# A graph network layer on one core: the matmul loop without its peeled steps, and loads that wait for the quad three ahead

## The reference, cut to what matters

```
agg = segment_sum(edge_attr, dst, num_segments=12500)      # 200000 x 128 f32, dst sorted
h = maximum(layernorm(x), 0)                               # 12500 x 128 f32
h = relu(concat(h, agg) @ W1 + b1)
h = relu(h @ W2 + b2)
h = h @ W3 + b3
out = x + layernorm(h) * ln_w + ln_b
```

## Time and profile before

| | us |
|---|---|
| median of three runs | 317.98 |
| the profiled execution, its own time | 318.58 |
| its span | 316.8 |
| PE busy | 271.7 (86%) |
| DVE busy | 246.4 (78%) |
| first load issued | 0.74 |
| flag known, branch taken | about 19.8 |
| last edges issued | 293.68 |
| last output issued | 313.76 and after |

### The profile page before, as it was taken

The page is one execution under the profiler, slowest core; times in us unless marked ns, Lnnn a source line. Parts: engine busy times, 40 slices in busy tenths (PEclk is TensorE's granted clock), DMA queues, the critical chain, the costliest instruction groups (busy, mean ns, idle before and its releaser), DMA issues.

```text
span 316.8 us, 12734 instructions
## 1 busy us (share of the span) xinstructions
PE 271.7 (86%) x3927; PEld 185.0 (58%) x3927; DVE 246.4 (78%) x944; ACT 149.6 (47%) x407; POOL 179.0 (56%) x208
## 2 busy tenths in 40 slices
PE   2949998998998888888988888889888888898991
PEld 0726666665665566655665565656655656565570
DVE  4946588989787878877787888778777887878885
ACT  1442555555544445455444454554443545544632
POOL 8636555566555656655555656555556565555431
PEclk9978999999999999999999999999999999999998
DMA  7999999999999999999999999999999999999994
GB/s 245 343 380 371 372 373 372 373 373 373 373 373 373 373 374 373 373 373 373 378 381 378 382 380 379 379 383 379 380 381 379 382 381 380 380 383 380 383 397 153
DMA packets 81855, 116.50 MB, mean 368 GB/s; under 512 B 5712, under 2 KB 81840, under 8 KB 81840
## 3 DMA queue, kind: packets, MB, share of 16 engines
q1 hardware_dynamic: 80826, 115.86, 103.2%
q10 hardware_dynamic: 1014, 0.46, 0.5%
HBM read 109.90 MB, written 6.40 MB: 367 GB/s over the span
## 4 chain that ended last, share of the span: by engine, by line
SPq 55%; PE 14%; issue 12%; DMA 11%; DVE 6%; ACT 0%; DVEq 0%; POOL 0%; POOLq 0%
SPq L295 43%; DMA ring<-in_edge_attr 9%; PE part_ps L438 6%; SPq L322 5%; SPq L290 5%; PE place_ps L449 3%; DMA dst_i<-in_dst 1%; PE hid_ps L466 1%; SPq L331 1%; PE hid_ps L483 1%; PE hid_ps L473 1%; PE y_ps L489 1%; DVE onehot L878 1%; DVE local L900 1%; DVE least L898 1%
## 5 line engine op out<-in xcount | busy, mean ns | idle before, releaser
L800 POOL TENSOR_SCALAR place<-iota,rows_at 128x128 f32<-128x128 f32 x131 | 104.9, 804 | 104.2 <-PE place_ps L449 95.0
L438 PE MATMUL part_ps<-ring,onehot 128*32 128x128 f32 x3120 | 113.4, 279 | 26.7 <-DMA ring<-in_edge_attr 25.8
L438 PEld LDWEIGHTS part_ps<-ring,onehot 128*32 128x32 f32 x3120 | 78.4, 110 | 72.6 <-issue 50.1
L954 DVE TENSOR_TENSOR agg<-place_ps,agg 128x128 f32 x131 | 38.0, 290 | 50.8 <-PE place_ps L449 49.0
L449 PE MATMUL place_ps<-place,part 128*128 128x128 f32 (+1 forms) x262 | 64.4, 328 | 2.6 <-POOL place L800 2.3
L808 POOL TENSOR_TENSOR xs<-xs,vecs 128x384 f32 (+2 forms) x33 | 54.8, 1662 | 19.4 <-ACT h L669 19.4
L878 DVE TENSOR_TENSOR onehot<-iota,local_t 128x768 f32<-128x768 f32 x66 | 63.5, 963 | 0.3 <-issue 0.3
L655 ACT ACTIVATE part<-part_ps 128x128 f32<-128x128 f32 x131 | 35.0, 268 | 48.4 <-PE part_ps L438 46.8
L449 PEld LDWEIGHTS place_ps<-place,part 128*128 128x128 f32 (+1 forms) x262 | 39.8, 190 | 29.1 <-issue 22.1
L669 ACT ACTIVATE h<-xs,x_shift,x_rstd 128x128 f32 (+2 forms) x98 | 41.3, 483 | 2.4 <-DVE x_shift L871 2.4
L685 ACT ACTIVATE hid<-hid_ps,b1s 128x384 f32<-128x384 f32 (+1 forms) x33 | 19.0, 577 | 45.4 <-PE hid_ps L473 45.4
(11 more groups left out here) (86 smaller groups left out, 201.9 us busy)
## 6 DMA issues: line engine op xcount, KB each, us to landing
ring<-in_edge_attr SPq DMA_DIRECT2D x260, 384.0 KB, 8.8
xs<-in_x SPq DMA_DIRECT2D x32, 192.0 KB, 8.5
out_x<-xs SPq DMA_DIRECT2D x11, 384.0 KB
out_x<-xs SPq DMA_DIRECT2D x16, 72.0 KB
dst_i<-in_dst SPq DMA_DIRECT2D x1, 768.0 KB
out_x<-xs SPq DMA_DIRECT2D x8, 48.0 KB
ring<-in_edge_attr SPq DMA_DIRECT2D x1, 192.0 KB, 8.7
out_x<-xs SPq DMA_DIRECT2D x1, 192.0 KB
```

What stands on the lines that cost most here:

```text
L438: last = nc.tensor.matmul(part_ps[par_q % 2][s * WIN:(s + 1) * WIN, 0:D], onehot[:, oct_par, first + s, j, :], e[:, s, j * D:(j + 1) * D], ...
L800: nc.gpsimd.tensor_scalar(place[:, par_q % 2, :], iota[:, 0:P], rows_at[:, k:k + 1], None, ALU.is_equal).then_inc(place_ready, 1)
L954: nc.vector.tensor_tensor(v, place_ps[par_q % 2][:, 0:P], v, ALU.add).then_inc(added, 1)
```

## The change

PE's loop takes steps 0 to 29 in 15 rounds, and no step stands alone. For this, DVE raises `y_evacuated` by one at the start, and those that wait for it wait for one more. Ahead of the branch, PE waits for the last copy of `local_t` and does 20 matmuls of 32 rows' columns into a bank that nothing reads. SP's loop is cut in two: steps 1 to 4 as they were, and steps 5 to 12, in which SP waits, ahead of each quad's two loads, until the quad three before has landed on all engines, and raises a semaphore that nobody waits for.

```
+UNDERWAY = 3
+SPARE = 20
+LEVEL_FROM = 2
...
+                    def few_underway(turn, pairs):
+
+                        n = turn - UNDERWAY
+                        sp.wait_ge(edges_loaded[n % RING], LANDED * (pairs + n // RING + 1))
+                        sp.sem_inc(sp_went_on, 1)
...
                         load_x(i + XAHEAD, (par + XAHEAD) % 2, pairs + (par + XAHEAD) // 2)
                         for k in range(4):
+                            if level:
+                                few_underway(4 * par + RING + AHEAD + k, pairs)
                             reload(4 * i + RING + AHEAD + k, (4 * par + AHEAD + k) % RING)
...
-                    with sp.Fori(0, ROUNDS - STORED_EARLY) as t:
+                    with sp.Fori(0, LEVEL_FROM) as t:
                         step(2 * t + 1, 1, t)
                         step(2 * t + 2, 0, t + 1)
+                    with sp.Fori(LEVEL_FROM, ROUNDS - STORED_EARLY) as t:
+                        step(2 * t + 1, 1, t, level=True)
+                        step(2 * t + 2, 0, t + 1, level=True)
...
-                    pe.wait_ge(y_evacuated, g)
+                    pe.wait_ge(y_evacuated, g + 1)
...
+                pe.wait_ge(local_t_ready, ROWT)
+                for _ in range(SPARE):
+                    nc.tensor.matmul(hid2_ps[0:WIN, 0:WIN], ident[:, 0:WIN], ident[:, 0:WIN], start=True, stop=True)
...
-                    step(0, 0, 0)
-                    with pe.Fori(0, (STEPS - 3) // 2) as t:
+                    with pe.Fori(0, (STEPS - 1) // 2) as t:
+                        step(2 * t, 0, t)
                         step(2 * t + 1, 1, t)
-                        step(2 * t + 2, 0, t + 1)
-                    step(STEPS - 2, 1, (STEPS - 2) // 2)
...
+                dve.sem_inc(y_evacuated, 1)
...
-                        dve.wait_ge(y_evacuated, g + 1)
+                        dve.wait_ge(y_evacuated, g + 2)
```

More of the change, by code:

```diff
@@ L189, in gnn_kernel @@
         added = sem("added")
+        sp_went_on = sem("sp_went_on")
         dve_went_on = sem("dve_went_on")
@@ L336, in fast, with step @@
                         reload(q, q % RING)
-                    def step(i, par, pairs, g=None, parts=()):
+                    def few_underway(turn, pairs):
+                        n = turn - UNDERWAY
+                        sp.wait_ge(edges_loaded[n % RING], LANDED * (pairs + n // RING + 1))
+                        sp.sem_inc(sp_went_on, 1)
+                    def step(i, par, pairs, g=None, parts=(), level=False):
                         load_x(i + XAHEAD, (par + XAHEAD) % 2, pairs + (par + XAHEAD) // 2)
                         for k in range(4):
+                            if level:
+                                few_underway(4 * par + RING + AHEAD + k, pairs)
                             reload(4 * i + RING + AHEAD + k, (4 * par + AHEAD + k) % RING)
```

## The result

| | us |
|---|---|
| before, median of 8 runs | 318.14 (317.53 to 318.57) |
| after, median of 8 runs | 319.06 (318.64 to 319.35) |
| ratio, 95% interval | 1.0028 (1.0017 to 1.0038) |
| forecast | 317.2 (316.2 to 318.4), faster |

The forecast had the direction wrong, and the time lies outside its range. The profiled execution of the changed kernel took 318.87 us.

What follows compares the result with a forecast made beforehand. The prediction took the DMA engines to bound the kernel, with the end set by the last quads landed plus a tail. It summed 317.98 - 0.8 (moved code fetch) + 0 (waiting loads) = 317.2 us, range 316.2 to 318.4.

Steps and rivals of the forecast that it cites:

- Loads that wait: SP's waits in steps 5 to 12: the last engine never runs dry, so 0, bounds -1.0 to +6 us.
- The 1 us from issue to data: In SP's held loads: first data about 1 us after issue, against 4.2 us of work left on the last engine.
- PE's part: PE's loop end moves by -165 instructions, so no code fetch hits the last quads: -0.8 us, bounds 0 to -0.8.
- evened out: Rival on SP's waits: the last engine gains what leading ones leave, quads land up to 1 us sooner; 316.3 us, 12%.
- the rates by share: DMA rates per full share, 360 and 350 with few engines against 352 with all: an engine alone is no faster.
- DMA-bound, end = last quads and a tail: Whole kernel: DMA share 1.06 from about 16 to 310 us; the end is the last quads landed, plus a tail.
- The 0.8 us in step 29 is the price of a code packet: Fetch of PE's code at 289:290 holds one DMA engine 1.1 us; quads 125 to 129 and the end come 0.8 late.
- Where the packets fall: PE's instruction packets after the change: four before 50 us, none between 60 and 302, the next after 306.8.
- Small matmuls: The 20 matmuls take 1.9 us, hidden in PE's idle time until 21.01, and may keep its 2.4 GHz clock: nothing gained.
- The jump, `y_evacuated`: One jump more at PE's loop end, up to 0.77 us of stall covered; `y_evacuated` raised on both sides: nothing from either.
- Starving: Rival on SP's waits: data comes later than the 4.2 us left, each of 32 quads costs; 318.8 us at 4.25, 8%.
- SP's waits for PE, "all of it before 31 us": SP waited for PE, for a ring slot, 6 times, 3.8 us in all, before 31 us, with DMA share still 1.06.

Runs made afterwards that it cites:

- sp_only: The kernel before with only SP's part of the change (loop cut in two, wait for the quad three before in steps 5 to 12): 319.10 us, ratio 1.0028.
- sp_no_hold: As `sp_only`, but waiting for the quad eight ahead (`UNDERWAY` 8 for 3), so that no wait ever holds: 318.33 us, 0.9992.
- the pair with few stores: `sp_only` and `sp_no_hold` without the 11 double stores at the end (groups 8 to 29 of the output not written): 319.0 and 318.22 us.
- after_no_hold: The changed kernel with `UNDERWAY` 8 in place of 3, so that its waits never hold: 318.02 us, ratio 0.9996.
- hold_one_loop: The changed kernel with SP's loop not cut in two; the wait stands in steps 1 to 12 and SP's code is shorter: 318.94 us, ratio 1.0026.
- after_again: The changed kernel itself measured once more, beside its variants: 318.71 us, ratio 1.0013.
- pe_only_again: A repeat of the kernel with only PE's part of the change (15-round loop, 20 small matmuls, `y_evacuated`), SP's code as before: 317.95 us, ratio 0.9996.
- after_hold_four: The changed kernel with SP waiting for the quad four ahead instead of three (`UNDERWAY` 4): 318.20 us, ratio 1.0001.
- hold_stored: The changed kernel with the wait in steps 13 to 28, where stores stand between the loads, and not in steps 5 to 12: 318.72 us, 1.0013.
- hold_eight_quads: The changed kernel with the wait in steps 11 and 12 only, so 8 quads are held back and not 32: 318.41 us, ratio 0.9997.
- no_hold_again: A repeat of the changed kernel with `UNDERWAY` 8, whose waits never hold: 318.38 us, ratio 0.9996.
- after_in_turn: The changed kernel, with POOL waiting for the step's second one-hot matrix before its bias operation: 317.97 us, ratio 0.9998.
- pe_only_in_turn: Only PE's part of the change, SP as before, with POOL waiting for the one-hot matrix before its bias operation: 317.81 us, ratio 0.9992.
- POOL's new wait: In three follow-up kernels POOL waits for DVE's one-hot matrix before adding its bias: 317.84 (`before_in_turn`), 317.81 (`pe_only_in_turn`) and 317.97 us (`after_in_turn`).
- pe_no_spare: Only PE's part of the change, SP as before, but without the 20 small matmuls (`SPARE` 0): 318.05 us, ratio 0.9995.
- few_stores_hold: `sp_only` without the 11 double stores of groups 8 to 29 behind the last load: 319.0 us, ratio 1.0037.
- before_in_turn: The kernel before, with POOL waiting for the step's second one-hot matrix before its bias operation: 317.84 us, ratio 0.9989.

## Why the prediction was wrong

**The step that failed** is the term "Loads that wait": "So 0", with "The leading engines may run dry for some tenths" priced at nothing. Three pairs differ in the one constant `UNDERWAY`, 3 against 8: `sp_only` less `sp_no_hold` 0.77, the pair with few stores 0.78, `after` less `after_no_hold` 1.04 (two sessions). Each interval leaves out zero. Against a kernel without the waits, whose SP code is shorter too, `hold_one_loop` and `after_again` are 0.99 and 0.76 above `pe_only_again`. The exceptions are `after_again` less `after_hold_four` 0.51, `hold_stored` 0.34 and `hold_eight_quads` 0.03 above `no_hold_again`, and `after_in_turn` less `pe_only_in_turn` 0.16, whose intervals all hold zero. So the hold of 32 quads costs about 0.8 us in the kernels without POOL's new wait. That it does is shown; how it does is in part my reading.

The term rested on two things. That the last engine doesn't run dry and decides when a quad lands was right during the stretch. That the leading engines' idle time is therefore worth nothing was not: it takes away a lead, and which engine is last can change later. The 1 us from issue to data was also too short, by the 2.6 us estimated above; the leading engines lost more than some tenths (in `after` the spread fell from 3.90 us at quad 33 to 2.22 at quad 65).

**The sum.** PE's part had -0.8 and measured -0.1 to -0.3 by the ratios, the hold had 0 and measured about +0.8: 318.14 - 0.2 + 0.8 = 318.7, where 319.06 came. The rest is within what such differences are known to.

**Where the loss comes back**, by the table: eight held traces against eleven others (the nine of the table's upper half, `pe_no_spare` and `pe_only_again`). Each is one execution, so this is what fits them and no experiment of its own.

- During the hold the last engine gains: quads 33 to 64 take 69.04 to 69.48 us where loads are held in steps 5 to 12 or 11 and 12, against 69.55 to 69.61. This is the rival "evened out", at a third of its size: the last engine got on a little faster while others idled, which the rates by share had spoken against.
- The price is that quad 129's mean landing goes from 299.2 to 300.1, and the spread at quad 65 from 3.3 to 4.7 down to 2.2 to 2.9 (3.67 in `hold_stored`, which holds only later). The engines have done less by then.
- Then, at some of the later code packets, another engine becomes the last. SP's code at 157: 9.71 and 9.56 us for quads 64 to 68 in `after` and `sp_only`, 9.02 to 9.12 with the same packet in three other held kernels, 8.93 to 9.04 without a hold. PE's code at 290 in `sp_only`: 1.2 us more between quads 124 and 125. PE's code at 299.2 in `few_stores_hold`: 9.69 for quads 125 to 129. SP's code at 296.8 or 300.2 in `hold_one_loop` and `hold_stored`: 9.39 and 9.33. Without a hold it is 8.95 to 9.02, also in the five kernels with a packet of PE near 299.
- In `after` that is a single engine: quad 66's last increment comes 0.73 us behind the last but one, in quad 65 it was 0.01. But SP's packet held its engine for 0.35 us only, and the landing lost 0.75. What makes up the rest no trace here shows.
- Those that escape at 157 lose some slowly among the stores: quads 68 to 124 take 126.90 to 127.03 us in five of them, 126.43 to 126.79 without a hold. `after` and `sp_only`, which lost at 157, have a spread of 3 again and lose nothing here (126.64, 126.55).

For `after` against `after_no_hold` the columns add up to the last landing: 0.36 at quad 33 (there before the hold, chance), -0.22, +0.75, +0.21, 0, +0.05, so 1.15 by rounding for 301.78 - 300.64 = 1.14. The share of each term changes from run to run.

**The late landing isn't all.** With PE's part, the six held traces have a last landing of 301.55 on average and a span of 316.9; the seven others 300.99 and 316.0. Of the 0.9 us, 0.56 is landing; the rest comes behind it, mostly in the three traces with the slip of DVE and POOL. That the hold makes the slip likelier is not shown: three of six against none of seven may be chance, and with few stores it occurs with and without a hold. The profiled execution of `after` has no slip.

**Point by point.**

- *DMA-bound, end = last quads and a tail*: right. Span less the last landing of quad 129 is 14.6 to 15.5 us in 15 of 17 traces of the table, and 16.0 and 15.9 in the two where the slip is largest.
- *The 0.8 us in step 29 is the price of a code packet*: the landings fit the mechanism, and the term was mis-sized. In `before` quad 125's last increment stands 0.84 us behind the last but one, 0.36 in quad 124: one engine. The same packet at 290 cost 0.82 in `before` (2.85 us for 2.03), 0 in `before_in_turn` and `sp_no_hold`, 0.5 in both kernels with few stores, 1.2 in `sp_only`: on average 0.5. The next packet, near 299, cost 0.7 in `few_stores_hold` and nothing in the five others. I had taken one draw for the rule. PE's part, worth -0.8 in the sum, has ratios worth -0.1 to -0.3 us in five kernels that hold nothing back, each with 1 in its interval. That it is even below 0.5 isn't explained.
- *Where the packets fall*: right. Four before 50 us, none to 302, the next at 304.7 (forecast 306.8). I counted PE's code and not SP's, whose packet at 157 was unforeseen.
- *Small matmuls*: right. Around the branch in `after`:

```profile
18.23 1.43 PE L527 MATMUL hid_ps<-ident 128*32 128x32 f32 x40
20.66 0.46 PE L464 MATMUL place_ps<-place,part 128*128 128x128 f32 x2 [1.00 <-POOL place L816]
```

  They take 1.43 us (1.9 estimated) inside PE's idle time; the granted clock in 20:22 goes from 0.52, mostly the 1.2 GHz level, to 1.00, the 2.4 GHz level; taking them out (`pe_no_spare`) costs nothing measurable.
- *The jump, `y_evacuated`*: nothing seen of either.
- *Starving*: it didn't come about, since with three quads under way the last engine doesn't run dry. It was nearer than the working had it: with two it costs 0.5 us a quad.
- *SP's waits for PE, "all of it before 31 us"*: misread. Three of the six, 1.9 of the 3.8 us, lie between 31 and 40 us; the share was 1.06 there too, so nothing hangs on it.

**What stays open.** How the 0.8 us splits between later code packets, the slow loss among the stores and the slip; why `after_in_turn` shows almost no loss; why the mean landing of `hold_eight_quads` is the latest of all and its median is not; and what spreads a kernel's runs over 1 to 3 us.

## What to carry to other kernels

When 16 DMA engines share each load, the last one sets the landing, and by these traces the lead of the others is what absorbs a code packet or uneven stores later: a throttle that leaves the leading engines idle spends it, even though no quad lands late at the time. If loads must be held back, leave enough under way that the DMA share doesn't move at all (four quads here, 3.1 MB; with three the rate fell by 1 to 2%). And a stall seen in one profiled execution is one draw: before removing it, look whether a second execution has it.

## What the runs showed of the hardware that I had not expected

- The engines reach the same load at different times, and keep their distance: without a hold a quad's 32 increments spread over 3.3 to 4.7 us (about 1.05 of it between its two halves), and from 60 to 290 us this changes by no more than about 0.5 us in a kernel.
- A code packet of 8 KB held one engine for 0.35 us (2.2% of 16 engines in 1 us), and twice a landing went late by 0.6 to 0.75 us just behind it.
- With the loop cut in two and waits in it, a packet of that queue came at 153 to 173 us, in the middle of the loads.
- Of a POOL and a DVE operation that start within 0.08 us of each other one takes 0.8 us longer, and 0.02 us decides which. When it is DVE's, PE reached the last quad 0.67 us later in three of five traces.
